# Loading layer 1's weights first and finding both weight maxima in one chain

## The reference

```python
def _cin_layer(xi, x0, W, b):
    Wr = W.reshape(Fi, F0, -1)
    out = jnp.einsum('nie,nje,ijo->noe', xi, x0, Wr) + b[None, :, None]
    return jax.nn.relu(out)
e = jnp.stack([tbl_0[ids[:, 0]], ..., tbl_47[ids[:, 47]]], axis=1)     # 512 x 48 x 32
xs = [e]
for W, b in ((W1, b1), (W2, b2), (W3, b3)):        # 48*48, 128*48, 128*48 rows of 128
    xs.append(_cin_layer(xs[-1], e, W, b))
z = jnp.concatenate(xs, axis=1).sum(axis=-1)
h = jnp.maximum(jnp.concatenate([z, dense_ctx], axis=1) @ W_top1 + b_top1, 0.0)
h = jnp.maximum(h @ W_top2 + b_top2, 0.0)
y = h @ W_top3
```

## Time and profile before

| | |
|---|---|
| median of 3 runs | 2483.61 us (2477.33 to 2484.41) |
| the profiled execution's own time | 2483.18 us |
| its span | 2481.3 us |
| busy in the span | PE 96%, DVE 91%, ACT 81%, POOL 81%, PEld 52% |
| mean granted TensorE clock | 0.983 of full |

### The profile page before, as it was taken

How to read it: one execution, slowest core, us unless ns; L and a number is a source line. 1 busy time by engine, 2 the same in 40 slices (tenths; PEclk the granted TensorE clock), 3 DMA queues, 4 the chain that set the end, 5 groups by cost and what they waited for, 6 DMA issues and landing times.

```text
span 2481.3 us, 67324 instructions
## 1 busy us (share of the span) xinstructions
PE 2371.5 (96%) x13024; PEld 1300.3 (52%) x13024; DVE 2253.5 (91%) x9408; ACT 2003.9 (81%) x7526; POOL 2005.8 (81%) x2006
## 2 busy tenths in 40 slices
PE   1399999999999999999999999999999999999998
PEld 0255555555555555555555555555555555555553
DVE  3589999999999999999999999999999999999995
ACT  1578888888888888888888888888888888888884
POOL 7178888888788888888878888888877777777773
PEclk7699999999999999999999999999999999999999
DMA  5000000000000000000000000000000000000000
GB/s 168 5 11 11 11 11 11 11 11 9 10 10 11 11 10 12 11 11 11 9 9 11 12 11 11 11 11 12 9 9 9 9 10 9 10 9 8 9 10 3
DMA packets 113451, 34.36 MB, mean 14 GB/s; under 512 B 107860, under 2 KB 111575, under 8 KB 113400
## 3 DMA queue, kind: packets, MB, share of 16 engines
q1 hardware_dynamic: 107256, 30.73, 5.6%
q0 software_dynamic: 6144, 3.16, 0.9%
HBM read 12.82 MB, written 0.00 MB: 5 GB/s over the span
## 4 chain that ended last, share of the span: by engine, by line
PE 93%; DVE 1%; issue 0%; DMA 0%; SPq 0%; ACT 0%; DVEq 0%
PE y L430 79%; PE m L420 11%; PE m L409 3%; DVE acc L746 1%; PE m L485 0%; PE y L485 0%; PE y L492 0%; DMA xT<-lo 0%; DVE ends L746 0%; PE y L498 0%; DVE msum L755 0%; DVE ends L760 0%; DVE pooled L799 0%; SPq L263 0%; DVE mp L779 0%
## 5 line engine op out<-in xcount | busy, mean ns | idle before, releaser
L430 PE MATMUL y<-whi,xT 128*128 128x512 f16 x6144 | 1990.3, 379 | 11.2 <-DMA xT<-lo 8.1
L528 ACT ACTIVATE work<-y,xc 128x128 f32<-128x128 f32 x5632 | 1597.3, 378 | 368.1 <-PE y L430 332.4
L746 DVE SCALAR_TENSOR_TENSOR acc<-y,xc,acc 128x128 f32<-128x128 f32 x5632 | 1680.5, 342 | 67.7 <-PE y L430 50.0
L324 POOL TENSOR_TENSOR part<-part,work 128x512 f32<-128x512 f32 x896 | 1138.1, 1270 | 204.7 <-ACT work L528 122.2
L430 PE MATMUL y<-wlo,xT 128*128 128x512 f16 x3072 | 1164.6, 379 | 0.0
L430 PEld LDWEIGHTS y<-whi,xT 128*128 128x128 f16 x6144 | 600.5, 98 | 633.6 <-issue 25.4
L430 PEld LDWEIGHTS y<-wlo,xT 128*128 128x128 f16 x3072 | 300.8, 98 | 241.0 <-issue 0.6
L420 PEld LDWEIGHTS m<-wsq,work 128*128 128x128 f32 x2304 | 355.1, 193 | 103.8 <-issue 20.0
L320 POOL TENSOR_TENSOR part<-work 128x512 f32<-128x512 f32 x256 | 326.6, 1276 | 61.8 <-ACT work L528 58.8
L420 PE MATMUL m<-wsq,work 128*128 128x128 f32 x2304 | 366.2, 278 | 2.5 <-DVE zst L725 2.5
L286 POOL DMA_INDIRECT emb<-tbl,ids_sb x192 | 185.4, 966 | 43.6 <-issue 27.2
(11 more groups left out here) (102 smaller groups left out, 1131.2 us busy)
## 6 DMA issues: line engine op xcount, KB each, us to landing
xT<-hi SPq DMA_TRANSPOSE x256, 2.2
xT<-lo SPq DMA_TRANSPOSE x256, 2.3
xx<-w SPq DMA_DIRECT2D x4, 768.0 KB, 5.4
emb<-tbl,ids_sb POOLq DMA_INDIRECT x192, 2.4
work<-w SPq DMA_DIRECT2D x4, 768.0 KB
x0T<-x0hl SPq DMA_TRANSPOSE x128
wt_sb<-W_top SPq DMA_DIRECT2D x1, 768.0 KB
w1s<-w_pair SPq DMA_DIRECT2D x1, 640.0 KB
```

Of the source, the lines that this page charges most:

```text
L324: pool.tensor_tensor(a[:], a[:], p[:, m, :], ALU.add).then_inc(s, 1)
L430: ins = nc.tensor.matmul(dst[:], xT[layer][:, parity, a, :], w[layer][:, cols], start=i == 0, stop=i == 2)
L528: nc.scalar.activation(prods[layer][:, a, k * P:(k + 1) * P], bank[:, k * P:(k + 1) * P], ACT.Copy, scale=xc[layer][:, parity, j:j + 1]).t ...
L746: ins = nc.vector.scalar_tensor_tensor(dst, y, col, mine, ALU.mult, ALU.add)
```

## The change

SP issues layer 1's weights, `member` and the biases right behind `ids`, ahead of the eight quarters; `sel` goes behind the quarters and has a semaphore of its own. DVE does layer 1's additions first, then the four maxima of `w2`, then waits for the diagonal's matmuls and takes the maximum of `wsq`, then the four maxima of `w3`, and after that one chain carries both maxima: two transposes with one count, one reduction to two numbers, and so on with two columns in place of one. ACT waits for count 16 of `s_wchain` in place of 14, which is the end of that joint chain with `zunit`.

```diff
         def _(sp):
             sp.dma_start(ids_sb[:], ids.rearrange("(b p) f -> p b f", p=P)).then_inc(s_ids, 16)
+            sp.dma_start(w1s[:], w_pair).then_inc(s_in, 16)
+            sp.dma_start(w1b[:], w_pair_t).then_inc(s_in, 16)
+            sp.dma_start(member[:], pairs_of).then_inc(s_in, 16)
+            for l in range(3):
+                sp.dma_start(brow[:, l * P:(l + 1) * P], ...).then_inc(s_in, 16)
             for l, w in enumerate((w2, w3)):
                 for c in range(4):
                     ...
-            sp.dma_start(w1s[:], w_pair).then_inc(s_in, 16)
-            ...
+            sp.dma_start(sel[:], select).then_inc(s_sel, 16)
@@
         def _(pe):
             pe.wait_ge(s_const, 5)
-            pe.wait_ge(s_wchain, 9)
-            nc.tensor.transpose(misc[0][0:1, 0:P], wmax[:, 8:9], eye32[:]).then_inc(s_wpe, 1)
-            pe.wait_ge(s_wchain, 12)
-            nc.tensor.matmul(misc[0][:, 0:1], ones[:], wmaxr[:, 2:3], start=True, stop=True).then_inc(s_wpe, 1)
-            pe.wait_ge(s_in, 7 * 16)
+            pe.wait_ge(s_in, 6 * 16)
             nc.tensor.matmul(misc[1][:, 0:3 * P], ones[:], brow[:], start=True, stop=True).then_inc(s_wpe, 1)
-            pe.wait_ge(s_wchain, 13)
             pe.wait_ge(s_setup, 1)
             for k in range(KT):
                 ins = nc.tensor.matmul(misc[0][0:F, 0:P], member[:, k, :], w1s[:, k, :], start=k == 0, stop=k == KT - 1)
             ins.then_inc(s_wpe, 1)
-            ...
+            pe.wait_ge(s_wchain, 10)
+            for g in range(2):
+                ins = nc.tensor.transpose(misc[0][0:1, g * P:(g + 1) * P], wmax[:, 8 + g:9 + g], eye32[:])
+            ins.then_inc(s_wpe, 1)
+            pe.wait_ge(s_wchain, 13)
+            nc.tensor.matmul(misc[1][:, 0:2], ones[:], wmaxr[:, 4:6], start=True, stop=True).then_inc(s_wpe, 1)
+            pe.wait_ge(s_sel, 16)
             pe.wait_ge(s_setup, SETUP)
@@
-            act.wait_ge(s_wchain, 14)
+            act.wait_ge(s_wchain, 16)
@@
+            dve.wait_ge(s_in, 6 * 16)
+            nc.vector.tensor_tensor(w1s[:], w1s[:], w1b[:], ALU.add).then_inc(s_setup, 1)
+            dve.wait_ge(s_setup, 1)
+            nc.vector.tensor_scalar(wsq[:], w1s[:], 0.5, None, ALU.mult).then_inc(s_setup, 1)
+            dve.wait_ge(s_wpe, 1)
+            nc.vector.tensor_copy(bcin[:]..., misc[1][:, 0:3 * P]).then_inc(s_setup, 1)
+            raw_max(0)
+            dve.wait_ge(s_wpe, 2)
             dve.wait_ge(s_setup, 2)
             nc.vector.scalar_tensor_tensor(wsq[0:F, 0, :], misc[0][0:F, 0:P], -0.5, w1s[0:F, 0, :], ...)
             dve.wait_ge(s_setup, 4)
             nc.vector.tensor_reduce(wmax[:, 9:10], wsq[:]..., op=ALU.max, apply_absolute_value=True)...
+            raw_max(1)
+            dve.wait_ge(s_wchain, 9)
+            nc.vector.tensor_reduce(wmax[:, 8:9], wmax[:, 0:8], axis=AX.X, op=ALU.max).then_inc(s_wchain, 1)
+            dve.wait_ge(s_wpe, 3)
+            nc.vector.tensor_reduce(wmaxr[:, 0:2], misc[0][0:1, 0:2 * P].rearrange("p (g n) -> p g n", g=2), ...)
+            ...
+            nc.vector.reciprocal(winv[:], wpow[:]).then_inc(s_wchain, 1)
             nc.vector.tensor_scalar(zunit[:], wpow[:, 1:2], SQUARE ** -2, None, ALU.mult).then_inc(s_wchain, 1)
-            dve.wait_ge(s_wchain, 21)
+            dve.wait_ge(s_wchain, 15)
             nc.vector.tensor_scalar(wsq[:], wsq[:], winv[:, 1:2], None, ALU.mult).then_inc(s_setup, 1)
```

## The result

The changed kernel took 2458.88 us, median of 5 (2458.32 to 2460.06), against 2483.61 (2477.33 to 2484.41) for the kernel before: a ratio of 0.9906, interval 0.9893 to 0.9919, or 24.7 us less. The forecast was 2458.7. The profiled execution took 2460.06 with a span of 2458.2, so its span is 23.1 us shorter than before's 2481.3.

The account below looks back on a forecast made before the run. PE bounds the whole span (93%), so only the first tile's start can move, down to the gathers' floor. Gain 25.5 less 1.0 for collisions is 24.5; 2483.2 less 24.5 is 2458.7 us, range 2455 to 2484.

Parts of the forecast that it names:

- The floor: First block's gathers on POOL: complete at 65.0, plus 0.6 spread, so first tile not before 65.6; largest gain 25.5 us.
- collisions: Gathers on POOL slowed beside DVE's SBUF-only operations: 0 to 1.9 us, taken as 1.0.
- the 2.5: Last gather's delay in us if each colliding DVE operation were added in full, the Trainium skill's objection.
- Steps on DVE and ACT: Prologue: layer 1's data in at 9.1, ACT starts at 31.1, DVE ends at 57.3, then waits for gathers.
- PE's counts: Prologue: counts late between 31.6 and 69.1, by 30.5 and 2.2 us, cause unknown; those before 28.4 prompt.
- two late counts: Kernel before's prologue: the diagonal's count (L391) late by 30.5 us and L396's by 2.2 us.
- A: Rival: the diagonal's matmuls take 34.4 us to their count at any time; gain 2.7 to 6.1, time 2479; chance 0.20.
- B: Rival: PE's counts held from about 30 us until gathers almost through; gain 0.7, time 2482.5; chance 0.11.
- C: Rival: the hold also takes in the diagonal's early count; 11 to 14 us slower, 2495.5; chance 0.12.
- The sum: Whole kernel: 2483.2 less 24.5 gives 2458.7 us.

Follow-up runs that it names:

- e10: Changed kernel with the last 12 of the first block's 48 gathers replaced by plain loads: 2449.36 us, ratio to the kernel before 0.9959.
- e11: Changed kernel with the quarters of w2 and w3 and all loads behind them issued only once the diagonal's count has come: 2458.72 us.
- e2: Kernel before with POOL's gathers held until L653 is done: 2488.05 us.
- e8: Kernel before with POOL stopping after 24 of the first block's 48 gathers until L653 is done: 2464.51 us.
- e4: Changed kernel with the diagonal's ten matmuls held until 24 gathers have landed: 2496.09 us.
- e6: Changed kernel with the old order of the loads, layer 1's inputs behind the quarters again: 2472.8 us.
- e1: Kernel before with the context's and tower's loads issued only after layer 1's setup is done: 2485.0 us.
- e3: Kernel before with ACT's first operation held until L653 is done: 2464.16 us.
- e5: Kernel before with the new order of the loads alone, both chains of maxima as before: 2486.69 us.
- e7: Kernel before with ACT's first operation waiting for the same PE count, the diagonal's, as DVE's L653: 2487.67 us.
- e12: Kernel before with only one of the diagonal's ten matmuls, 2 passes in place of 20: 2458.62 us.

## Why the prediction was right, and what it left out

**The floor.** The forecast hung on the gathers ending near 65.0 plus 0.6 for the spread, and on 1.0 for collisions. Landed at 65.8, the first tile at 66.30 against 66.6: right, and e10 and e11 show from both sides that it is the gathers. The collisions moved the last gather by 0.7 us (63.35 against 62.64), so the 1.0 was a little high and the 2.5 that a full block of each operation would have given is far from what this trace shows.

**Steps on DVE and ACT.** Layer 1's data in at 8.8 (forecast 9.1), L642 at 18.4 (19.2), ACT at 29.9 (31.1), the last subtraction ended at 56.0 (57.3). The data came 0.3 us sooner, and each four maxima took 6.8 to 6.9 us in place of 7.2. None of it mattered, since 8.6 us of slack lay behind.

**PE's counts.** The joint chain's two came 0.04 us after the modelled ends of their matmuls (27.70 and 29.40). The diagonal's was due at 15.0 and wanted at 18.38, so it was at most 3.4 us late. That was the part without a cause in the prediction, with 0.43 laid on rivals. In the kernel before it names two late counts; a third, of L394, was 1.3 us late (modelled end 64.36, L661 at 65.63), and its sums allow for that. Of the rivals, A (the matmuls take that long wherever they run) falls with e2 and with the changed kernel itself. B and C named the gathers, and e2 and e8 show that they take part; e4 came out at C's price. In the changed kernel neither came true: the diagonal's count fell due at 15 and the joint chain's last at 29.4. There is luck in that. The forecast had no reason why a count due at 29.4 should be prompt, and in e6 one due at 30.7 was 11.4 us late. No run here shows what sets the limit, nor whether the change would have gained its 25 us on another such occasion.

**The sum.** 24.8 at the first tile less 1.7 behind it is 23.1 in the span; the forecast had 24.5 and nothing behind. The 1.7 are within what one execution differs from another: from the first tile to the end the 14 traces take 2389.7 to 2392.3 us, the changed kernel 2391.9 and 2390.8, and e1, in the old order, 2392.3. In 13 of them that time grows with how late the granted clock rises (the first matmul of L430 that takes 0.38 us in place of 0.6 comes 21.5 us behind the first tile's start where it is 2389.7, and 24.3 where it is 2391.9 or 2392.3). How late it rises doesn't follow from how long PE had been idle: that was 41.6 us before L409 in both traces of the changed kernel, and 29.6 in e1. The medians, 24.7 apart, agree better than the profiled pair.

**What it left out.** It took the lateness as a property of the kernel. Three runs within 7 us suggested that, and no view could have refuted it. In two of five places the kernel before is at the floor of the gathers by itself, and in the one of them where the changed kernel ran as well the change is worth nothing (0.9999). The 25 us were measured in the one place with a late count in which both ran. That the changed kernel took 2459 in both of its places makes it look the safer of the two, but e4 and e6 show that its order isn't proof against a late count.

**Open.** What passes between the gathers and PE's count isn't settled. With all gathers running, the lateness of the diagonal's count was 30.5, 29.1, 11.4, 23.0, 33.8, 11.4 and 33.1 us (kernel before, e1, e3, e4, e5, e6, e7). Nor is it simply held until the gathers end: in e3 and e6 it came in the middle of them, in e5 and e7 some 5 and 2 us after the last one was issued. In e3 and e6, the two with 11.4, one gather beside DVE's additions had taken 2.3 us before it, where the longest in the other five took 1.25 to 1.90; nothing here tells whether that belongs together. Nor are running gathers enough, or needed: in e3, e5 and e8 some other counts due between 28 and 46 us came 0.04 us after their matmuls with gathers running (in e3 the next one, due at 46.8, was 3.4 late), and in e7 two counts due at 67.4 and 69.9, with the last gather issued at 62.4, were still 1.3 and 0.9 us late. That the gathers matter to the diagonal's count rests on one execution each of e2 and e8, against seven without a pause. Whether it needs the other transfers to be quiet, and whether it grows with the number of passes, was tried in e11 and e12 and not answered.

## What to carry to other kernels

Where an engine waits far past the end of what it waits for and the trace can't name the releaser, look for what else runs in that stretch, and try it out by pausing that for the length of the wait; here one wait in POOL's program got back 20.7 us in one execution. Where such a wait shows, put the small steps that cross between engines before the stretch in which it shows (here the one in which only indirect DMAs ran), and leave for that stretch the long work that needs no such step. And run the kernel before again in a second place before a gain of 1% is booked: the same pair of kernels gave 0.9906 in one and 0.9999 in another.

## What the runs showed of the hardware

- The count of the diagonal's last matmul, due between 30.7 and 40.4 us, came 11.4 to 33.8 us after that matmul's modelled end in seven executions in which POOL issued gathers every 1.25 us. With the gathers paused it came 4.8 us after it (e8) and with them held 0.04 us (e2). Other counts of PE came 0.04 us after their matmuls with the gathers running (29.40 in the changed kernel, 45.53 in e3).
- ACT and DVE, waiting for that same count, started within 0.05 us of each other (e7).
- A gather that takes 0.95 us by itself took 1.19 to 1.64 in three places of the changed kernel, beside DVE's copies and tensor_scalars. Its 48th was issued 0.7 us later than in the kernel before, which had one such gather, of 1.33.
- The time of one kernel differed by 25 us, 1%, between groups of runs on different chips and at different times, while the runs beside one another stayed within 3 us (7 for the kernel before in the result; the one run of 3419.8 left out).
